# A graph kernel whose last quarter chunk is packed into four columns, and whose last sums and first node groups are handled in another order

## The chip, the cores and the metric

The kernel runs on one core of one Trainium2 chip. The core has five engines that run their own instruction streams: TensorE (PE, matrix multiplies; its weight loads are shown as PEld), VectorE (DVE), ScalarE (ACT), GpSimd (POOL) and SyncE (SP, which here only issues DMAs). Engines wait for each other through semaphores; DMAs are carried by 16 shared DMA engines. The metric is the device time of one execution, in microseconds (us); below, "ns" is written where nanoseconds are meant.

## The reference

A graph network layer over 6250 nodes and 200000 edges with 64 features each; `dst` is sorted, `src` is not.

```python
in_agg = jax.ops.segment_sum(edge_feat, receivers, num_segments=N_NODES)   # by dst
out_agg = jax.ops.segment_sum(edge_feat, senders, num_segments=N_NODES)    # by src
to_updater = jnp.concatenate([in_agg, out_agg, node_feat], axis=1)         # 6250 x 192
h = jax.nn.relu(to_updater @ W1 + b1)                                      # 192 -> 256
x = _layernorm(x + (h @ W2 + b2), axis=-1)                                 # 256 -> 64
```

## The kernel before, in words

Edges are taken in 98 chunks of 2048. A chunk lies in SBUF as 128 partitions by 16 columns of 64 features; the first 1024 edges fill columns 0 to 7 (partition p holds edges 8p to 8p+7), the other 1024 columns 8 to 15. Columns go through the kernel in quads of four. 200000 edges leave 1344 for the last chunk: its first half is full, and of its second half 40 partitions by 8 columns hold the last 320 edges (`LAST_PARTS` is 40); the rest of the half is zeroed features, with node numbers repeated from real edges.

- **Sums by dst** are made by windows: for each half chunk a one-hot matrix of 64 nodes is multiplied by the features on PE (48 matmuls, `sum_windows`), and DVE adds the window to `aggT[0:64]` (`add_window`).
- **Sums by src, directly**: for a quad PE multiplies the features by a matrix of equal node numbers (`same`), so that every edge's row holds the sum over the column's edges of the same node; ACT copies this from PSUM to `payload`, DVE writes row numbers to `target`, and POOL issues one indirect scatter-add DMA for each column (`add_chunk`) into one of four tables in HBM (`out_tab`). The first 2 and the last 18 chunks do this for all four quads, the 78 between for one quad only.
- **Sums by src, shared**: the other 12 columns of the 78 middle chunks are first added into slots (`slot_round`), written to HBM, and read back during the last 18 chunks, where PE adds slot tiles to nodes in seven pairs of node groups (`sum_tiles`, line 1529, 64x64 matmuls with 448 columns). After each pair ACT copies four sums out of PSUM (`flush`) and PE folds them together, one half after the other (`fold`), for ACT to put into `aggT[64:128]` (`put_sums`).

In the last chunk (c = 97, the 18th unit) PE runs, for each of four quads, the next quad's spread of node numbers (line 1491), the 12 matmuls of the quad (lines 1578 and 1580) and some slot tiles; then the windows, and 792 slot matmuls without a break. Then comes the tail, in which nothing is left to overlap with the chunks:

1. SP waits for each table's last scatter-add (`SCATTERED`) and loads its part of node groups 0 and 1 (512 nodes each; there are 12 groups of 512 and one of 106), and then each later group once the sum two groups before has been made.
2. PE folds the last pair: both halves go through the same PSUM bank, so that the second fold waits until ACT has copied out the first (`s_folded`).
3. For each node group g: DVE adds the four tables (`sum_tables`, two instructions), PE transposes the result (`sum_turned`), DVE adds it to `aggT` (`add_tables`, two instructions). PE multiplies by W1: the node's own features (`x_turned`, `hidden_own` in two parts) and the sums (`hidden_sums`); ACT rectifies; PE multiplies by W2 (`outputs`); ACT adds the bias (`biased`); PE transposes back (`back`); DVE adds x and normalizes (line 1389 and on), with the power on POOL, which also issues the store.

The order on each engine is the order in which the code is written. Ahead of the loop over groups stand both parts of `hidden_own` of groups 0 and 1, both `sum_turned`, both `hidden_sums` on PE, and on DVE `sum_tables` and `add_tables` of group 0, the same of group 1, and `sum_tables` of group 2:

```python
for b in range(2):          # DVE
    sum_tables(b, b)
    add_tables(b, b)
sum_tables(2, 0)
```

At the start SP loads the node numbers (`rows_i`, 98 rows of 2048, for src and dst) with four DMAs each, the last row in two pieces (1344 real numbers, 704 repeated ones). ACT turns them to floats for PE to transpose, and DVE takes their minima and maxima.

## Time and profile before

| | |
|---|---|
| median of 3 runs (range) | 1465.55 us (1464.92 to 1467.31) |
| the profiled execution | 1469.09 us, of which the profile spans 1467.2 us |
| PE busy in the span | 1366.5 us (93%) |
| DVE, ACT, POOL busy | 1351.0, 1016.1, 1173.4 us |
| middle chunks (150 to 815 us) | PE busy 652.93 of 665.00 us |
| last 18 chunks, most of them (850 to 1300 us) | PE busy 448.02 of 450.00 us |
| from the last slot matmul to the first layer norm | 1379.30 to 1401.64 us |
| PE busy from 1380 to 1400 us | 14.12 of 20.00 us, mean clock 0.83 |
| layer norm groups, to the last store's issue | 1401.64 to 1459.79 us |

A row of a timeline has the start, the busy time, the engine and line, the operation with output and inputs, and how many instructions were merged; in brackets stands how long the engine had been idle before, and what released it ("issue" is nothing that the profile shows). fp32 matmuls appear as two records each. A row of stretches has, for PE, PEld, DVE, ACT and POOL in this order, the busy time with the number of instructions, then PE's granted clock (1.00 is 2.4 GHz, 0.50 is 1.2 GHz), the busy share of the DMA engines and what they moved in GB/s.

### The profile page before, as it was taken

The numbers are of one execution on the slowest core, as the hardware profiler recorded it, in microseconds if no ns is written. First come the engines' busy times: TensorE is split into PE (matmuls) and PEld (weight loads), VectorE is DVE, ScalarE is ACT, GpSimd is POOL, SyncE is SP. The second block draws the span as 40 slices with busy tenths as digits, with TensorE's granted clock in tenths as the row PEclk, the third lists the DMA queues.
The fourth block names the chain that finished last, engine by engine and source line by source line (L and its number), as shares of the span: only waits on it lengthen the run. The fifth ranks groups of instructions, "written<-read, shape, count | busy, mean of one in ns | idle before, by whom it ended". The sixth has DMA issues, their size and how long they took to land.

```text
span 1467.2 us, 64101 instructions
## 1 busy us (share of the span) xinstructions
PE 1366.5 (93%) x23716; PEld 1064.3 (73%) x23716; DVE 1351.0 (92%) x3564; ACT 1016.1 (69%) x2201; POOL 1173.4 (80%) x667
## 2 busy tenths in 40 slices
PE   3557999999999999999999899999999999999896
PEld 2347999999999999999999566556656565665443
DVE  6987999999999999999999899989999999998576
ACT  6425777777777788887777666776766667676343
POOL 2888888888888888888888688888888888888533
PEclk9969999999999999999999899999999999999998
DMA  9226777777777777779888777776767677666441
GB/s 302 33 15 145 194 194 191 190 195 191 185 185 185 192 195 193 193 192 218 213 211 213 189 181 198 173 186 167 191 166 193 167 185 188 162 172 157 86 129 49
DMA packets 216734, 255.53 MB, mean 174 GB/s; under 512 B 99469, under 2 KB 179356, under 8 KB 216392
## 3 DMA queue, kind: packets, MB, share of 16 engines
q1 hardware_dynamic: 123482, 223.88, 46.7%
q0 software_dynamic: 92960, 28.90, 22.2%
q8 instruction: 105, 1.72, 0.5%
q10 hardware_dynamic: 144, 0.67, 0.2%
q14 instruction: 43, 0.35, 0.1%
HBM read 143.18 MB, written 110.21 MB: 173 GB/s over the span
## 4 chain that ended last, share of the span: by engine, by line
PE 45%; DMA 25%; issue 13%; POOL 12%; DVE 3%; ACT 1%; POOLq 1%; DVEq 0%; ACTq 0%
PE psum L1529 32%; DMA out_tables<-payload,target 24%; POOL out_tables L670 12%; PE psum L1507 3%; PE psum L1676 1%; PE psum L1491 1%; PE psum L1484 1%; PE psum L1580 1%; PE psum L1667 1%; PE psum L1578 1%; PE psum L1688 1%; PE psum L1553 1%; PE psum L1554 1%; DMA cst<-in_consts 1%; DVE to_node L1188 0%
## 5 line engine op out<-in xcount | busy, mean ns | idle before, releaser
L670 POOL DMA_INDIRECT out_tables<-payload,target x632 | 1140.0, 1804 | 223.3 <-issue 187.9
L1507 PE MATMUL psum<-parts,to_slot 128*128 128x194 bf16 x6552 | 589.9, 248 | 7.5 <-ACT slots_out L765 7.5
L1507 PEld LDWEIGHTS psum<-parts,to_slot 128*128 128x128 bf16 x6552 | 555.4, 98 | 24.3 <-issue 8.0
L1529 PE MATMUL psum<-to_node,slots_in 64*64 64x448 bf16 x9828 | 481.2, 351 | 3.3 <-ACT halves_sum L847 2.0
L1529 PEld LDWEIGHTS psum<-to_node,slots_in 64*64 64x64 bf16 x9828 | 284.7, 107 | 178.2 <-DVE to_node L1188 6.1
L765 ACT ACTIVATE slots_out<-psum 128x388 bf16<-128x388 f32 (+1 forms) x936 | 367.5, 474 | 57.0 <-PE psum L1507 49.4
L1149 DVE TENSOR_SCALAR to_slot<-iota_h,slot 128x896 bf16<-128x896 f16 x940 | 377.7, 455 | 0.1
L1188 DVE TENSOR_SCALAR to_node<-iota_h,slot_rel 128x448 bf16<-128x448 f16 x819 | 267.0, 343 | 3.8 <-PE psum L1529 3.2
L1188 DVE TENSOR_SCALAR to_node<-iota_rows,slot_rel 128x448 bf16<-128x448 f16 x546 | 237.1, 434 | 0.0
L784 ACT ACTIVATE payload<-psum 128x256 f32<-128x256 f32 x158 | 61.0, 386 | 207.7 <-PE psum L1580 193.0
L816 ACT ACTIVATE to_node<-apart 128x448 bf16<-128x448 bf16 x273 | 149.0, 575 | 68.3 <-PE psum L1529 67.3
L808 ACT ACTIVATE apart<-iota_h,slot_rel 128x448 bf16<-128x448 f16 x273 | 167.5, 663 | 0.5 <-DVE slot_rel L1160 0.5
L1108 DVE TENSOR_TENSOR rest<-feat,parts 128x1024 f32<-128x1024 f32 x98 | 119.9, 1223 | 22.4 <-ACT parts L744 21.3
L1216 DVE TENSOR_TENSOR same<-psum,cols_code 128x512 bf16<-128x512 f32 x158 | 109.0, 690 | 21.2 <-PE psum L1491 11.7
L1113 DVE TENSOR_TENSOR parts<-rest,parts 128x1024 bf16<-128x1024 f32 x98 | 118.8, 1212 | 1.9 <-ACT parts L754 1.9
L754 ACT ACTIVATE parts<-rest 128x1024 bf16<-128x1024 f32 x98 | 107.5, 1097 | 1.2 <-DVE rest L1108 1.2
L744 ACT ACTIVATE parts<-feat 128x1024 bf16<-128x1024 f32 x98 | 104.5, 1066 | 2.0 <-PE psum L1484 1.9
L1484 PEld LDWEIGHTS psum<-onehot,parts 128*64 128x64 bf16 x4704 | 87.2, 113 | 19.8 <-issue 19.8
L1484 PE MATMUL psum<-onehot,parts 128*64 128x64 bf16 x4704 | 100.8, 198 | 0.0
L1578 PE MATMUL psum<-parts,same 128*128 128x65 bf16 x632 | 79.8, 198 | 13.7 <-issue 8.3
L1580 PE MATMUL psum<-parts,same 128*128 128x64 bf16 x1264 | 84.3, 197 | 0.0
L1578 PEld LDWEIGHTS psum<-parts,same 128*128 128x128 bf16 x632 | 61.0, 100 | 27.4 <-issue 21.6
(129 smaller groups left out, 812.7 us busy)
## 6 DMA issues: line engine op xcount, KB each, us to landing
slot_tiles<-slots_out SPq DMA_DIRECT2D x78, 1018.5 KB
feat<-in_edge_attr SPq DMA_DIRECT2D x195, 256.0 KB
slots_in<-slot_tiles SPq DMA_DIRECT2D x40, 970.0 KB
slots_in<-slot_tiles SPq DMA_DIRECT2D x40, 921.5 KB
out_tables<-payload,target POOLq DMA_INDIRECT x632
out_tables<-zeros POOLq DMA_DIRECT2D x4, 1600.0 KB
feat<-out_tables SPq DMA_DIRECT2D x48, 128.0 KB, 2.2
slots_in<-slot_tiles SPq DMA_DIRECT2D x14, 242.5 KB
```

Source lines behind the costliest of these rows:

```text
L670: e.indirect_dma_start(out_tab, at, payload[b][:, t, :], None, element_offset=k * TABLE_ROWS * D, compute_op=ALU.add).then_inc(s_tab[k], 16)
L765: e.activation(slots_out[b][:, g:g + n, m, :], ps_share[r % BANKS][:, 0:n * SLOT_W].rearrange("p (g w) -> p g w", w=SLOT_W), ACT.Copy).the ...
L808: e.activation(apart[:, n % APARTS, :], iota_h[:, 0:HOT], ACT.Abs, bias=slot_rel[p % RING][:, k:k + 1], scale=-1.0).then_inc(s_apart, 1)
L816: e.activation(to_node[:, node_buf(g, i), :], apart[:, n % APARTS, :], ACT.Relu, bias=1.0, scale=-1.0).then_inc(s_to_node_act, 1)
L1108: e.tensor_tensor(rest[:, :, :], feat[b][:, :, :], parts[b][:, :, 1:1 + D], ALU.subtract).then_inc(s_rest, 1)
L1113: e.tensor_tensor(parts[b][:, :, 1 + 2 * D:1 + 3 * D], rest[:, :, :], parts[b][:, :, 1 + D:1 + 2 * D], ALU.subtract).then_inc(s_lo, 1)
L1149: last = e.tensor_scalar(to_slot[m][:, k, :], iota_h[:, :], slot[:, bass.ds(s, 1), MINI * m + k:MINI * m + k + 1].rearrange("p a k -> p (a ...
L1188: e.tensor_scalar(hot, numbers, slot_rel[p % RING][:, k:k + 1], None, ALU.is_equal).then_inc(s_to_node, 1)
L1484: last = e.matmul(ps_win[b][h], parts[b][:, t, 1 + k * D:1 + (k + 1) * D], onehot[b][:, t // 2, :, t % 2], start=(j == 0 and k == 0), stop ...
L1507: last = e.matmul(ps_share[r % BANKS][:, o:o + SLOT_W], to_slot[m][:, k, g * P:(g + 1) * P], parts[b][:, SHARE_FROM + MINI * m + k, 1:], s ...
L1529: return e.matmul(ps_share[bank_no + h][cols, 0:HOT], slots_in[p % RING][rows, j - PART_FROM[p], D * k:D * (k + 1)], to_node[rows, node_bu ...
L1578: e.matmul(ps_pay[:, o:o + D + 1], w, parts[b][:, t, 0:1 + D], start=True, stop=False)
```

## The change

- The last 320 edges lie in 80 partitions by 4 columns (8 to 11). Columns 12 to 15 of the last chunk hold zeros, and its fourth quad is left out: on PE (12 matmuls and one spread), DVE (`same`), ACT (two copies) and POOL (four scatter-adds). The windows still cover all 16 columns.
- So that the node numbers fit, the last row of `rows_i` is loaded in three pieces: 1024 numbers; 80 times four numbers, each four written twice side by side (a source that is repeated, runs of four numbers, 16 bytes); and 384 repeated ones. That is five DMAs each for src and dst, ten instead of eight.
- The two folds of the last pair go to two PSUM banks (`both`), so that the second no longer waits for the first one's copy.
- In the tail DVE adds the tables of groups 0 and 1 before it adds either to `aggT`, and adds group 2's there too, ahead of the loop. PE has group 0's `sum_turned` between the two groups' `hidden_own`, group 0's `hidden_sums` before group 1's `sum_turned`, group 2's `x_turned` before group 0's `outputs`, and group 2's `sum_turned` right behind it. ACT copies group 2's `x_turned` before `biased` of group 0.

```diff
-LAST_PARTS = (LAST_EDGES - HALF_EDGES) // HALF
-PAD = CHUNK - LAST_EDGES
+LAST_ROWS = (LAST_EDGES - HALF_EDGES) // QUAD
+PAD = (P - LAST_ROWS) * HALF
...
+        FINAL = Mode(0, COLS - QUAD, window=True, sums=True)
...
-        SCATTERED = 16 * ((SHARE_FROM * SHARE_CHUNKS + COLS * (N_CHUNKS - SHARE_CHUNKS)) // OUT_TABLES + 1)
+        SCATTERED = 16 * ((SHARE_FROM * SHARE_CHUNKS + COLS * (N_CHUNKS - SHARE_CHUNKS) - QUAD) // OUT_TABLES + 1)
...
-                chunk(c, c // 2, c % 2, SUMMING, u)
+                chunk(c, c // 2, c % 2, FINAL if is_final(c) else SUMMING, u)
...
-                e.dma_start(rows_i[n][N_CHUNKS - 1:N_CHUNKS, 0:LAST_EDGES], last).then_inc(s_row[n], 16)
-                e.dma_start(rows_i[n][N_CHUNKS - 1:N_CHUNKS, LAST_EDGES:CHUNK],
+                e.dma_start(rows_i[n][N_CHUNKS - 1:N_CHUNKS, 0:HALF_EDGES], last[:, 0:HALF_EDGES]).then_inc(s_row[n], 16)
+                with nc.allow_non_contiguous_dma(reason="the last quarter chunk's rows, four by four"):
+                    e.dma_start(rows_i[n][N_CHUNKS - 1:N_CHUNKS, HALF_EDGES:CHUNK - PAD].rearrange(
+                                    "a (p k j) -> a p k j", k=HALF // QUAD, j=QUAD),
+                                last[:, HALF_EDGES:LAST_EDGES].rearrange("a (p k j) -> a p k j", k=1, j=QUAD).to_broadcast(
+                                    [1, LAST_ROWS, HALF // QUAD, QUAD])).then_inc(s_row[n], 16)
+                e.dma_start(rows_i[n][N_CHUNKS - 1:N_CHUNKS, CHUNK - PAD:CHUNK],
                             last[:, LAST_EDGES - PAD:LAST_EDGES]).then_inc(s_row[n], 16)
...
-                    same_nodes(c, b, c, mode, q)
+                    if q < len(mode.quads):
+                        same_nodes(c, b, c, mode, q)
...
             def group(g, b):
-                biased(g, b)
                 if g == 0:
                     out_of_transposes(2, 0)
+                biased(g, b)
...
-                if g + 2 <= GROUPS:
+                if 3 <= g + 2 <= GROUPS:
                     add_tables(g + 2, b)
...
             for b in range(2):
                 sum_tables(b, b)
+            for b in range(2):
                 add_tables(b, b)
             sum_tables(2, 0)
+            add_tables(2, 0)
...
-                e.wait_ge(s_folded, 2 * g + (h + 1))
-                e.matmul(ps_fold[c % 2], fold_mat[:, :], halves_sum[h][:, :], start=True, stop=False)
-                e.matmul(ps_fold[c % 2], fold_mat[:, :], halves_sum[2 + h][:, :], start=False, stop=True).then_inc(s_fold, 1)
+                both = h if is_last(g) else 0
+                e.wait_ge(s_folded, 2 * g + (h + 1) - both)
+                to = ps_fold[(c + both) % 2]
+                e.matmul(to, fold_mat[:, :], halves_sum[h][:, :], start=True, stop=False)
+                e.matmul(to, fold_mat[:, :], halves_sum[2 + h][:, :], start=False, stop=True).then_inc(s_fold, 1)
```

PE from the two last folds on, before; L1667 is `hidden_own`, L1648 `sum_turned`, L1676 `hidden_sums`, L1688 `outputs`, L1638 `x_turned`, L1696 `back`:

```order
L1553 MATMUL psum<-halves_sum,fold_mat 64x448
L1554 MATMUL psum<-halves_sum,fold_mat 64x448
L1667 MATMUL psum<-parts,w1xx 128x256 x8
L1648 MATMUL psum<-cst,rest 128x128 x4
L1676 MATMUL psum<-aggT,w1io 128x512 x4
L1688 MATMUL psum<-payload,w2s 64x256 x4
L1638 MATMUL psum<-cst,xs 128x128 x4
L1696 MATMUL psum<-cst,onehot 128x128 x2
L1648 MATMUL psum<-cst,rest 128x128 x2
```

The same stretch of PE after the change; L1686 is `hidden_own`, L1667 now `sum_turned`, L1695 `hidden_sums`, L1707 `outputs`, L1657 `x_turned`, L1715 `back`:

```order
L1572 MATMUL psum<-halves_sum,fold_mat 64x448
L1573 MATMUL psum<-halves_sum,fold_mat 64x448
L1686 MATMUL psum<-parts,w1xx 128x256 x4
L1667 MATMUL psum<-cst,rest 128x128 x2
L1686 MATMUL psum<-parts,w1xx 128x256 x4
L1695 MATMUL psum<-aggT,w1io 128x512 x2
L1667 MATMUL psum<-cst,rest 128x128 x2
L1695 MATMUL psum<-aggT,w1io 128x512 x2
L1657 MATMUL psum<-cst,xs 128x128 x2
L1707 MATMUL psum<-payload,w2s 64x256 x4
L1667 MATMUL psum<-cst,rest 128x128 x2
L1657 MATMUL psum<-cst,xs 128x128 x2
```

The same matmuls are issued; group 0's transpose of sums has moved between the two `hidden_own`, group 0's `hidden_sums` ahead of group 1's transpose, and group 2's transposes ahead of and behind `outputs`. DVE in the tail, before; L1358 and L1363 are `sum_tables`, L1377 `add_tables`, L1389 the first row of a group's layer norm:

```order
L1358 TENSOR_TENSOR feat<-feat 128x512
L1363 TENSOR_TENSOR rest<-feat 128x256
L1377 TENSOR_TENSOR aggT<-aggT,psum 64x256 x2
L1358 TENSOR_TENSOR feat<-feat 128x512
L1363 TENSOR_TENSOR rest<-feat 128x256
L1377 TENSOR_TENSOR aggT<-aggT,psum 64x256 x2
L1358 TENSOR_TENSOR feat<-feat 128x512
L1363 TENSOR_TENSOR rest<-feat 128x256
L1389 TENSOR_TENSOR onehot<-xs,psum 128x256
```

And after the change, where L1373 and L1378 are `sum_tables`, L1392 `add_tables` and L1404 the layer norm's first row:

```order
L1373 TENSOR_TENSOR feat<-feat 128x512
L1378 TENSOR_TENSOR rest<-feat 128x256
L1373 TENSOR_TENSOR feat<-feat 128x512
L1378 TENSOR_TENSOR rest<-feat 128x256
L1392 TENSOR_TENSOR aggT<-aggT,psum 64x256 x4
L1373 TENSOR_TENSOR feat<-feat 128x512
L1378 TENSOR_TENSOR rest<-feat 128x256
L1392 TENSOR_TENSOR aggT<-aggT,psum 64x256 x2
L1404 TENSOR_TENSOR onehot<-xs,psum 128x256
```

Both groups' `sum_tables` now stand before the first `add_tables`, and group 2's `add_tables`, which stood inside group 0's layer norm, stands before it.

## Rows read from the trace of the kernel before

**Rows 1.** Stretches: start:end, length, busy per engine, PEclk, DMA share, GB/s.
```profile
850.00:1300.00 450.00, 448.02 (x9304) 272.80 (x9297) 427.65 (x1319) 308.70 (x607) 379.79 (x230) 1.00 0.71 180
```

**Rows 2.** Timeline, PE, last chunk: start, busy, engine, line, operation, count.
```profile
1334.57 0.39 PE L1491 MATMUL psum<-rows_code,ident_bf 98*128 98x512 bf16 x1
1334.80 0.20 PE L1578 MATMUL psum<-parts,same 128*128 128x65 bf16 x1
...
1338.76 0.20 PE L1578 MATMUL psum<-parts,same 128*128 128x65 bf16 x1
...
1339.23 0.59 PE L1553 MATMUL psum<-halves_sum,fold_mat 128*64 128x448 f32 x1
...
1341.65 37.65 PE L1529 MATMUL psum<-to_node,slots_in 64*64 64x448 bf16 x792
```

**Rows 3.** Timeline, POOL, the last scatter-add.
```profile
1379.51 1.55 POOL L670 DMA_INDIRECT out_tables<-payload,target  x1 [0.30 <-issue]
```

**Rows 4.** Timeline, from the last slot matmul to the first fold.
```profile
1379.35 1.85 ACT L847 ACTIVATE halves_sum<-psum 128x448 f32<-128x448 f32 x4 [5.61 <-PE psum L1529]
...
1382.98 0.63 PE L1638 MATMUL psum<-cst,xs 128*128 128x128 f32 x4 [3.68 <-issue]
...
1383.54 1.69 PE L1553 MATMUL psum<-halves_sum,fold_mat 128*64 128x448 f32 x2
```

**Rows 5.** The same timeline, second fold to first layer-norm input.
```profile
1387.30 0.69 DVE L1358 TENSOR_TENSOR feat<-feat 128x512 f32<-128x512 f32 x1 [12.86 <-DMA feat<-out_tables]
...
1387.35 0.97 PE L1553 MATMUL psum<-halves_sum,fold_mat 128*64 128x448 f32 x2 [0.63 <-ACT aggT L854]
...
1389.00 2.67 PE L1667 MATMUL psum<-parts,w1xx 64*128 64x256 f32 x16
...
1391.61 0.44 PE L1648 MATMUL psum<-cst,rest 128*128 128x128 f32 x2
1392.08 0.85 DVE L1377 TENSOR_TENSOR aggT<-aggT,psum 64x256 f32<-64x256 f32 x2 [3.63 <-PE psum L1648]
...
1394.17 0.69 PE L1648 MATMUL psum<-cst,rest 128*128 128x128 f32 x2 [2.13 <-DVE rest L1363]
...
1394.66 4.91 PE L1676 MATMUL psum<-aggT,w1io 128*128 128x512 f32 x8
...
1399.50 1.08 PE L1688 MATMUL psum<-payload,w2s 128*64 128x256 f32 x8
...
1401.64 0.42 DVE L1389 TENSOR_TENSOR onehot<-xs,psum 128x256 f32<-128x256 f32 x1 [4.70 <-PE psum L1696]
```

**Rows 6.** Stretches of 2 us with the granted clock.
```profile
1385.00:1387.00 2.00, 1.72 (x3) 0.23 (x1) 0.00 (x0) 0.24 (x1) 0.00 (x0) 0.50 0.48 141
...
1395.00:1397.00 2.00, 2.00 (x3) 0.68 (x2) 1.86 (x4) 0.33 (x1) 0.00 (x0) 0.50 0.78 230
```

**Rows 7.** The same timeline, start of group 1's tail on PE.
```profile
1405.40 0.41 PE L1638 MATMUL psum<-cst,xs 128*128 128x128 f32 x2 [1.18 <-DVE aggT L1377]
...
1406.08 1.88 PE L1676 MATMUL psum<-aggT,w1io 128*128 128x512 f32 x4
```

**Rows 8.** Chain that ended last, tail: start, us, what.
```profile
1415.85 1.72 PE psum L1676 x4
...
1420.65 1.72 PE psum L1676 x4
```

**Rows 9.** Timeline, start of the kernel.
```profile
9.32 1.91 ACT L732 ACTIVATE rows_f<-rows_i 98x2048 f32<-98x2048 int32 x1 [6.04 <-DMA rows_i<-in_src]
...
13.51 1.91 ACT L732 ACTIVATE rows_f<-rows_i 98x2048 f32<-98x2048 int32 x1
14.01 2.22 DVE L994 TENSOR_REDUCE lowest<-rows_i 98x2 f32<-98x2048 int32 x1
```

**Rows 10.** DMA packets of the first 14 us.
```profile
DMA packets 920, 3.27 MB, mean 233 GB/s; under 512 B 109, under 2 KB 109, under 8 KB 726
```

**Rows 11.** The page's DMA queues (packets, MB, share of 16 engines).
```profile
q0 software_dynamic: 92960, 28.90, 22.2%
```

More of the change, by code:

```diff
@@ L397, in quad_no @@
                 return QUADS * c
-            return c + (QUADS - 1) * FIRST if mode is SHARING else QUADS * c - (QUADS - 1) * SHARE_CHUNKS
+            if mode is SHARING:
+                return c + (QUADS - 1) * FIRST
+            return QUADS * c - (QUADS - 1) * SHARE_CHUNKS - (0 if mode.window else 1)
         def quad_buf(q, b, mode):
@@ L435, in summing_loop @@
                 c = END_SHARE + u
-                chunk(c, c // 2, c % 2, SUMMING, u)
+                chunk(c, c // 2, c % 2, FINAL if is_final(c) else SUMMING, u)
         def sums_before(mode, u):
             for g in range(NODE_PAIRS - 1):
-                if mode is SUMMING and u > 0 and SUM_FROM[u - 1] < (g + 1) * TILES <= SUM_FROM[u]:
+                if mode.sums and u > 0 and SUM_FROM[u - 1] < (g + 1) * TILES <= SUM_FROM[u]:
                     return g
@@ L544, in step @@
                                 slots_out[b][:, :, :, :].rearrange("p g m w -> p g (m w)")).then_inc(s_slot_out[b], 16)
-                if mode is SUMMING:
+                if mode.sums:
                     for k in range(RING, PARTS * NODE_PAIRS):
@@ L1550, in fold @@
                     e.wait_ge(s_wadd, HALVES * (c + 1) + 2)
[L1552 to L1554 removed]
+                both = h if is_last(g) else 0
+                e.wait_ge(s_folded, 2 * g + (h + 1) - both)
+                to = ps_fold[(c + both) % 2]
+                e.matmul(to, fold_mat[:, :], halves_sum[h][:, :], start=True, stop=False)
+                e.matmul(to, fold_mat[:, :], halves_sum[2 + h][:, :], start=False, stop=True).then_inc(s_fold, 1)
             def chunk(c, i, b, mode, at, d=None):
@@ L1708, in group @@
                 if g == 0:
-                    x_turned(2, 0)
+                    sum_turned(2, 0)
                 if g + 3 <= GROUPS:
@@ L1725, in _ @@
                 fold(NODE_PAIRS - 1, m, N_CHUNKS)
-            for b in range(2):
-                for k in range(2):
-                    hidden_own(b, b, k)
-            for b in range(2):
-                sum_turned(b, b)
-            for b in range(2):
-                hidden_sums(b, b)
+            for k in range(2):
+                hidden_own(0, 0, k)
+            sum_turned(0, 0)
+            for k in range(2):
+                hidden_own(1, 1, k)
+            hidden_sums(0, 0)
+            sum_turned(1, 1)
+            hidden_sums(1, 1)
             all_groups(e, group)
```

31 lines of the change are left out of this document (18 added, 13 removed).

## The prediction

> **What bounds the kernel now.** I read the stretches first, since the change touches the start, one chunk near the end and the tail, and each has a limit of its own. In the last 18 chunks PE is the engine that never rests: 448.02 of 450.00 us, at the full clock [rows 1]. So work taken from PE in the last chunk counts in full, and work taken from the others counts only if PE would have waited for it. The timeline of PE shows the last chunk: 792 slot matmuls end the stage without a gap, at 1341.65 + 37.65 = 1379.30 us [rows 2]. POOL, which had issued a scatter-add every 1.55 + 0.30 = 1.85 us, ends its last one at 1381.06 us [rows 3]. That looks like a tie in which the scatters are the later. The next rows decide it: what does each of the two release?
>
> - The scatters release the table loads and so `sum_tables` of group 0 on DVE, at 1387.30 us [rows 5], 6.24 us after POOL's end. But PE takes that sum only at 1391.61 us (L1648), because it is busy with the folds and with 16 records of `hidden_own` until then [rows 5]. The scatter chain ends 1391.61 - 1388.42 = 3.2 us early (`sum_tables` is 0.69 us and a second, smaller instruction, some 1.12 us together by the gap from 1387.30).
> - PE's end releases ACT's four copies (1.85 us) and, after 3.68 us in which PE waits for nothing that the profile shows (it reads the flag and branches), transposes and the first fold at 1383.54 us [rows 4].
>
> So the tail hangs on PE. In it stand two waits that matter. PE waits 0.63 us for ACT to copy the first fold [rows 5]. And at 1394.17 us it has stood 2.13 us for DVE, which does group 0's `add_tables` (0.85 us from 1392.08) and only then group 1's `sum_tables` [rows 5]. Behind this wait the clock is low: 0.50, that is 1.2 GHz, in 1395 to 1397 us, as it was in 1385 to 1387 behind the first pause [rows 6], and the eight records of `hidden_sums` take 4.91 us [rows 5] where four take 1.72 later on [rows 8]. From group 2 on PE sets the pace, one group every 1420.65 - 1415.85 = 4.80 us [rows 8]; this line starts at the `hidden_sums` of 1406.08 us, ahead of which PE waited 1.18 us for DVE's `add_tables` of group 2 [rows 7].
>
> **The change part by part.**
>
> *The quad left out, on PE.* The spread costs 1334.80 - 1334.57 = 0.23 us and the 12 matmuls 1339.23 - 1338.76 = 0.47 us [rows 2]. PE is the bound here, so 0.70 us. Ends: 0, if PE waited for one-hot tiles instead (DVE also loses one `same`, so it doesn't fall behind), and 0.70.
>
> *The quad left out, on POOL.* Four scatter-adds, 4 x 1.85 = 7.4 us [rows 3]. Their end moves to about 1373.7 us and both `sum_tables` become possible before PE's last matmul. What was late was never this chain, so I price it at nothing, with one condition: the new order wants both groups' table sums before group 0's `sum_turned`, some 1.6 us earlier than it stood. With the old scatters DVE would end them at 1387.30 + 2 x 1.12 = 1389.5 us, just at the point of need; the 7.4 us buy certainty there, not time. ACT's two copies and DVE's `same` go from engines that wait for PE: nothing.
>
> *The second bank.* The 0.63 us wait goes [rows 5]. The first fold ran at 1.2 GHz (four records from 1383.54 to the copy, near 3.2 us) and the second at the full clock (1387.35 to 1389.00, 1.65 us) [rows 5, 6]. If the clock rises as late as before, the second fold now begins below it. Ends: the full 0.63, or a loss of 1.65 - 0.63, about 1.0, if all of it runs at half the clock. I take 0.33: less than half of it is slowed, as the clock was back by 1387.35.
>
> *The order of the tail.* Before, from `hidden_own` (1389.00) to the first layer norm row (1401.64) are 12.64 us [rows 5]. Now, counted from `hidden_own`: half of it 1.30; group 0's transpose 0.25 of issue; the other half 1.30, under which DVE's 0.85 is hidden (0.44 + 0.85 against 0.25 + 1.30); `hidden_sums` of group 0 at the full clock 1.72 [rows 8], at 4.57. Group 1's transpose 0.44 and its `add_tables` 0.85 with two handovers of 0.05: 5.95, a wait of about 1 us in place of the 2.13. `hidden_sums` of group 1 1.72, at 7.67; group 2's two transposes about 0.33, at 8.0. `outputs` and what followed took 1401.64 - 1399.50 = 2.14 us [rows 5]; but DVE now has `add_tables` of group 2 ahead of the layer norm: `outputs` 1.01, transpose 0.44, add 0.85 and handover make 2.35. Sum 10.35, so 12.64 - 10.35 = 2.3 us. Of these about 1.3 are the low clock (three of the eight records at 0.86 instead of 0.43 us), the rest is the shorter wait.
>
> *The period's start.* The first layer norm row is then 0.70 + 0.33 + 2.3 = 3.3 us earlier. `add_tables` of group 2 no longer stands inside group 0, and the 1.18 us for which PE waited on it [rows 7] go in part: DVE still is the slower one for a group or two. Between 0 and 1.18 I take 0.6. The line of 4.80 us a group then starts 3.9 us earlier, and all later groups keep their instructions.
>
> *The loads at the start.* Ten DMAs for eight, and in two of them 160 runs of 16 bytes. The src numbers are awaited by ACT (9.32 us), the dst numbers by ACT at 13.51, where it didn't wait, and by DVE at 14.01 [rows 9]; so dst had landed by 13.51, and DVE has 0.5 us to spare. The trace has no such load. The nearest row for a small packet is that of the scatter-adds: 22.2% of 16 engines' 1467.2 us over 92960 packets is 56 ns each [rows 11]. Spread over 16 engines, 10 packets each, that is 0.56 us for one such DMA and 1.1 for both; less 0.5 spare, 0.6 us lost. On one engine it is 160 x 56 ns = 9 us each, 18 us for both. The lower end is 0, if small packets pass beside the large ones. In the first 14 us 109 packets are under 512 B [rows 10], though the single rows of before are runs of 2.8 to 8 KB: single rows are cut up and, most likely, spread. I take a loss of 0.3.
>
> The Trainium skill, "DMA: Bandwidth & Descriptors" (section "Why a DMA increments its semaphore by 16 and not by 1"), says that a DMA uses the largest number of engines up to 16 that divides the slowest dimension of both sides. With 80 or 160 there it would be 16, which speaks for the cheap end. [...] No row of this trace shows on how many engines a load ran.
>
> **Sum.** 0.70 + 0.33 + 2.3 + 0.6 - 0.3 = 3.6 us. The profiled execution took 1469.09 us, so 1465.5 (a span of 1463.6). It lay 3.54 us above the median of the timed runs; the same step from 1465.55 us gives 1462.0 us.
>
> **The rivals.**
>
> - *The clock stays low in the tail.* A pause of about 1 us remains ahead of group 1's `hidden_sums`, and 2.1 us were enough before [rows 5, 6]. Then the 1.3 us come back: 2.3 us gained, 1463.3. For it: the low stretch followed after a busy share of about half. Against it: PE is busy nearly without a break from 1383 on.
> - *The small terms fall short.* The folds bring nothing, DVE keeps the pace of the first groups, the start costs 0.8, the clock stays low: 3.6 - 0.3 - 0.6 - 0.5 - 1.3 = 0.9, 1464.7 us.
> - *The small load is slow.* If the 160 runs go through one DMA engine, dst lands up to 18 us later, src up to 9; DVE, busy without a gap from 14 us on, passes all but 0.5 on to the chunks. Half of the price, 9 us, gives 1465.5 + 8.5 - 3.9 = 1470.2 us. It decides as soon as the delay is over 0.5 + 3.9 = 4.4 us, or 27 ns a packet for both DMAs on one engine. Against it: rows 10.
> - *The scatters were the bound after all.* If the 3.68 us before PE's first transpose are in truth a wait for something on the scatter's side, up to 7.4 - 0.7 more is to be had; with PE then bound by ACT's copies, which end at 1381.20 [rows 4], at most 1382.98 - 1381.20 = 1.8 more: 1460.2 us. Against it: the table sums were 3.2 us early.
>
> **How the numbers follow.** Forecast 0.52; clock 0.20; small terms 0.13; slow load 0.08; scatters 0.07. A change below 0.2%, 2.9 us, can't be told from none by this kernel's runs, which puts the border at 1462.6 us, only 0.6 from the forecast. The forecast's own spread of about 1 us lies three quarters beyond it (0.39), with a quarter of the clock case (0.05) and the last case (0.06): faster 0.50. Slower needs 1468.5 us: 0.08 of the slow load and hardly anything else, 0.08. Same: 0.42. The range leaves out the slow load and part of the ends: 1460.2 to 1465.2 us.
>
> **What would show it.** The row L1529 of 792 ends 0.7 us earlier against the start of the last chunk. POOL's last scatter ends 5 us or more before it. The second L1572 of the last pair shows no wait for ACT. The two `hidden_sums` are apart, with 0.8 to 1.1 us of idle PE between them, and the granted clock from 1390 us on is 1.00. From PE's last slot matmul to the first L1404 are 19.7 us instead of 22.34; the period stays 4.80. At the start, DVE's first reduction stands at 14.0 to 14.6 us. I am wrong if that is past 16 us, if the clock is at 0.50 over 2 us of the tail, or if the gap from the last slot matmul to the first layer norm is as long as before.

## The result, and the profile after

Twelve timed runs each gave 1463.37 us (1460.10 to 1464.94) for the changed kernel and 1466.32 us (1463.58 to 1468.98) for the one before (among its twelve are the three that were known ahead): a ratio of 0.9976, with a 95% interval of 0.9967 to 0.9985, which is 3.5 us (2.2 to 4.8) gained. Forecast were 3.6. The profiled execution spans 1461.7 us instead of 1467.2; these 5.5 us are more than the timed runs show, and the experiments say why.

The last chunk on PE in the profile after (timeline, columns as before) answers to [rows 2]:

```profile
1335.34 0.20 PE L1597 MATMUL psum<-parts,same 128*128 128x65 bf16 x1
...
1339.30 0.59 PE L1572 MATMUL psum<-halves_sum,fold_mat 128*64 128x448 f32 x1
...
1341.72 37.65 PE L1546 MATMUL psum<-to_node,slots_in 64*64 64x448 bf16 x792
```

From the quad's first matmul to the last fold before the windows were 1339.23 - 1334.80 = 4.43 us and are 1339.30 - 1335.34 = 3.96: 0.47 us less, to the digit; the spread's 0.23 us are gone ahead of the quad. The slot matmuls end at 1379.37 us, where they ended at 1379.30. The 0.70 us are there, but this execution was some 0.75 us longer ahead of the last chunks: its first slot matmul stands at 817.97 instead of 817.22 us, though the start is equal (below). In nine profiled executions, those in which the kernel before takes 1466 to 1468 us (of the two kernels and of variants of them), the slot matmuls end between 1377.05 and 1380.50 us, so a span alone can't show 0.7 us.

The tail in the profile after, for [rows 3 to 5] and [rows 7]:

```profile
1373.18 1.55 POOL L683 DMA_INDIRECT out_tables<-payload,target  x1 [0.30 <-issue]
...
1379.67 0.69 DVE L1373 TENSOR_TENSOR feat<-feat 128x512 f32<-128x512 f32 x1 [5.16 <-DMA feat<-out_tables]
...
1380.73 0.68 DVE L1373 TENSOR_TENSOR feat<-feat 128x512 f32<-128x512 f32 x1
...
1382.64 0.63 PE L1657 MATMUL psum<-cst,xs 128*128 128x128 f32 x4 [3.27 <-issue]
...
1383.20 0.96 PE L1572 MATMUL psum<-halves_sum,fold_mat 128*64 128x448 f32 x2
...
1384.75 0.92 PE L1572 MATMUL psum<-halves_sum,fold_mat 128*64 128x448 f32 x2
...
1386.35 1.47 PE L1686 MATMUL psum<-parts,w1xx 64*128 64x256 f32 x8
...
1387.75 0.44 PE L1667 MATMUL psum<-cst,rest 128*128 128x128 f32 x2
...
1389.52 1.98 PE L1695 MATMUL psum<-aggT,w1io 128*128 128x512 f32 x4
...
1391.76 0.86 DVE L1392 TENSOR_TENSOR aggT<-aggT,psum 64x256 f32<-64x256 f32 x2 [2.68 <-PE psum L1667]
...
1392.67 1.98 PE L1695 MATMUL psum<-aggT,w1io 128*128 128x512 f32 x4 [0.95 <-DVE aggT L1392]
...
1397.19 0.42 DVE L1404 TENSOR_TENSOR onehot<-xs,psum 128x256 f32<-128x256 f32 x1
```

PE goes from the first fold into the second without a wait (1383.20 to 1386.35). The table sums, which DVE ended at 1388.4 us and 1394.1 before, are both done by 1381.9, so that the only wait left ahead of a `hidden_sums` is the 0.95 us for group 1's `add_tables`. From the last slot matmul to the first layer norm row are 17.82 us where there were 22.34; the forecast was 19.7. The folds account for 2.0 us of it (3.15 instead of the 5.13 that the forecast implies) and a shorter pause for 0.4 (3.27 instead of 3.68), while the order fell 0.5 short (10.84 instead of 10.35). The folds are short because the clock was up (stretches of 2 us, the granted clock third from the end):

```profile
1383.00:1385.00 2.00, 2.00 (x8) 0.77 (x7) 0.00 (x0) 0.70 (x3) 0.00 (x0) 1.00 0.90 278
...
1391.00:1393.00 2.00, 1.05 (x5) 0.50 (x4) 1.19 (x3) 1.12 (x2) 0.00 (x0) 1.00 0.00 0
1393.00:1395.00 2.00, 2.00 (x8) 0.86 (x8) 0.77 (x2) 1.00 (x2) 0.00 (x0) 1.00 0.09 30
```

It is 1.00 all through the tail. So the four fp32 products of the folds took 3.15 us, at about 0.39 us a record, where the first half of them ran at half the clock before [rows 4, 6]. The period behind is unchanged, 4.80 us a group, in the chain that ended last (start, length, what), as in [rows 8]:

```profile
1410.71 1.72 PE psum L1695 x4
...
1415.51 1.72 PE psum L1695 x4
```

And the start, for [rows 9]:

```profile
9.80 1.91 ACT L745 ACTIVATE rows_f<-rows_i 98x2048 f32<-98x2048 int32 x1 [6.52 <-DMA rows_i<-in_src]
...
13.97 2.29 DVE L1008 TENSOR_REDUCE lowest<-rows_i 98x2 f32<-98x2048 int32 x1 [0.47 <-DMA rows_i<-in_dst]
```

Src numbers came 0.48 us later and dst numbers at least 0.46 (before, ACT didn't wait for them at 13.51 us); DVE stood 0.47 us for them, and its first reduction is where it was, because its work on the constants had begun 0.9 us sooner in this execution. The first matmul of chunk 0 moved by 0.04 us.

### The profile page after: what moved, and what is told of

Same layout as the page of the kernel before. It is cut to its first block, busy times and chain, and to the rows that moved or that the text cites. A ratio compares the mean times of both kernels' runs of the same rounds, so it can differ in the third digit from the quotient of the medians.

```text
span 1461.7 us, 64069 instructions
## 1 busy us (share of the span) xinstructions
PE 1364.3 (93%) x23703; PEld 1062.9 (73%) x23703; DVE 1351.8 (92%) x3563; ACT 1015.8 (69%) x2199; POOL 1164.2 (80%) x663
## 3 DMA queue, kind: packets, MB, share of 16 engines
q8 instruction: 105, 1.72, 0.5%
## 4 chain that ended last, share of the span: by engine, by line
PE 44%; DMA 25%; issue 13%; POOL 13%; DVE 3%; ACT 1%; POOLq 1%; SPq 0%; DVEq 0%; ACTq 0%
PE psum L1546 31%; DMA out_tables<-payload,target 24%; POOL out_tables L683 13%; PE psum L1524 3%; PE psum L1508 1%; PE psum L1501 1%; PE psum L1695 1%; PE psum L1599 1%; PE psum L1686 1%; PE psum L1597 1%; PE psum L1707 1%; PE psum L1572 1%; DMA rows_i<-in_dst 1%; PE psum L1573 1%; DVE to_node L1202 1%
```

## The experiments

Ten variants ran, and the changed kernel twice more, in four groups, each on a chip of its own. Each ratio is against the kernel before on the same chip in the same group. On the chips of the first and third group the kernel before takes 1468 us; on those of the second (banks and order, eight fillers, early flag, the load that can't be cut evenly) and the fourth (late flag) 1519 to 1521 us, so only ratios go across. For the tail three distances are read from each profile, in us: from the last slot matmul to the transposes of x (pause), from the first fold to `hidden_own` (folds), and from there to the first layer norm row (order).

| kernel | ratio (95%) | pause | folds | order | POOL's end against the last slot matmul |
|---|---|---|---|---|---|
| before | 1 | 3.68 | 5.46 | 12.64 | +1.76 |
| changed | 0.9976 (0.9967 to 0.9985) | 3.27 | 3.15 | 10.84 | -4.64 |
| two banks alone | 0.9996 (0.9986 to 1.0006) | 3.34 | 4.84 | 13.17 | +5.60 |
| order alone | 0.9991 (0.9982 to 1.0001) | 3.07 | 5.53 | 11.55 | +5.92 |
| quad out alone | 0.9986 (0.9971 to 1.0001) | 3.12 | 6.37 | 11.63 | -2.42 |
| changed, again | 0.9973 (0.9963 to 0.9984) | 3.33 | 4.85 | 10.84 | -3.96 |
| banks and order | 0.9991 (0.9976 to 1.0006) | 3.53 | 4.35 | 10.85 | -1.77 |
| changed, eight fillers | 0.9968 (0.9954 to 0.9982) | 4.03 | 4.84 | 10.84 | -4.57 |
| changed, early flag | 0.9975 (0.9961 to 0.9989) | 2.99 | 5.68 | 10.84 | -7.01 |
| changed, load as 79 and 1 | 0.9980 (0.9966 to 0.9993) | 3.63 | 5.34 | 10.84 | -6.83 |
| changed, scatters back | 0.9976 (0.9963 to 0.9988) | 3.21 | 3.15 | 17.67 | +6.58 |
| changed, third time | 0.9971 (0.9956 to 0.9985) | 3.60 | 4.85 | 10.84 | +1.61 |
| early flag, 14 fillers | 0.9950 (0.9932 to 0.9967) | 3.07 | 3.15 | 10.83 | -1.95 |
| late flag, 14 fillers | 0.9965 (0.9953 to 0.9978) | 3.76 | 3.15 | 10.84 | -6.34 |

### The three parts, each alone, and the whole

Two banks alone:

```diff
-                e.wait_ge(s_folded, 2 * g + (h + 1))
-                e.matmul(ps_fold[c % 2], fold_mat[:, :], halves_sum[h][:, :], start=True, stop=False)
+                both = h if is_last(g) else 0
+                e.wait_ge(s_folded, 2 * g + (h + 1) - both)
+                to = ps_fold[(c + both) % 2]
+                e.matmul(to, fold_mat[:, :], halves_sum[h][:, :], start=True, stop=False)
```

> The kernel before with the two last folds in two PSUM banks and nothing else. Theory PE (the tail hangs on PE's chain, and the change saves 0.70 us by the quad, 0.3 to 0.6 by the folds, some 2.9 by the order): 0.3 to 0.6 us faster than before; in the profile no wait for ACT between the two folds, the rest of the tail as before, and 22.34 us from the last slot matmul to the first layer norm row become about 21.9. Rival theory clock (what the changed kernel's profile gained beyond the forecast, the folds in 3.15 us instead of 5.46, comes from the change): the folds take 3.2 us here too and 2 us are gained. Rival chance (the clock over the folds differs from execution to execution with no bearing on the change): the folds take 3.2 or 4.8 us, whichever the execution happens to have, and the timed gain stays 0.3 to 0.6.

Measured 0.6 us (a loss of 0.9 to a gain of 2.1). PE's timeline of this run:

```profile
1382.34 1.41 PE L1560 MATMUL psum<-halves_sum,fold_mat 128*64 128x448 f32 x2
...
1385.04 1.46 PE L1560 MATMUL psum<-halves_sum,fold_mat 128*64 128x448 f32 x2
...
1387.18 2.68 PE L1674 MATMUL psum<-parts,w1xx 64*128 64x256 f32 x16
...
1390.14 0.44 PE L1655 MATMUL psum<-cst,rest 128*128 128x128 f32 x2 [0.28 <-DVE rest L1368]
...
1393.00 5.28 PE L1683 MATMUL psum<-aggT,w1io 128*128 128x512 f32 x8
```

The second fold follows without a wait, and the folds take 4.84 us: 0.62 less than before, just the wait. The clock is low in most of them, and again low in `hidden_sums` (5.28 us). So two banks alone don't bring the full clock over the folds. From the last slot matmul to the first layer norm row are 21.91 us, as expected. One thing was not: POOL ended 5.60 us behind the last slot matmul, and PE waited 0.28 us for DVE's table sum. So late scatters can cost time in the old order too.

Order alone (the edits of the tail from the diff above, on PE, DVE and ACT):

```diff
             for b in range(2):
                 sum_tables(b, b)
+            for b in range(2):
                 add_tables(b, b)
             sum_tables(2, 0)
+            add_tables(2, 0)
```

> The kernel before with the new order of the tail on PE, DVE and ACT alone; four columns of scatters more than the changed kernel, one PSUM bank for both folds. Theory PE: 2.3 us sooner at the first layer norm row and 0.6 more by the third group, together 2.9 us; the table sums of both groups end at about 10 us behind the last slot matmul, just as PE wants them, so at most 0.3 of it is lost. Rival scatters (the quad's 7.4 us of scatters are what makes the order pay): group 0's transpose waits for DVE's table sums by 0.5 us or more, and less than 2 us are gained.

Measured 1.3 us (a loss of 0.1 to a gain of 2.6): fewer than the 2.9 expected. The timeline, all engines, and POOL's last scatter:

```profile
1388.30 1.47 PE L1669 MATMUL psum<-parts,w1xx 64*128 64x256 f32 x8
...
1389.04 0.69 DVE L1358 TENSOR_TENSOR feat<-feat 128x512 f32<-128x512 f32 x1 [14.85 <-DMA feat<-out_tables]
...
1390.25 0.44 PE L1650 MATMUL psum<-cst,rest 128*128 128x128 f32 x2 [0.48 <-DVE rest L1363]
...
1392.19 1.98 PE L1678 MATMUL psum<-aggT,w1io 128*128 128x512 f32 x4
```

```profile
1383.41 1.55 POOL L670 DMA_INDIRECT out_tables<-payload,target  x1 [0.30 <-issue]
```

Here POOL ended 5.92 us behind the last slot matmul, and DVE could begin the table sums only at 1389.04 us. PE waited 0.48 us ahead of group 0's transpose. From `hidden_own` to `hidden_sums` are 3.89 us instead of 3.17. That is the rival's wait, at its lower end (it said 0.5 us or more), and less than 2 us were gained, as it said.

Quad out alone (the changed kernel with folds and tail order as before):

```diff
+        FINAL = Mode(0, COLS - QUAD, window=True, sums=True)
...
-                chunk(c, c // 2, c % 2, SUMMING, u)
+                chunk(c, c // 2, c % 2, FINAL if is_final(c) else SUMMING, u)
```

> The kernel before with the last 320 edges in four columns and without the last quad; ten loads of node numbers instead of eight; folds and tail order as before. Theory PE: 0.70 us on PE in the last chunk, 0.0 lost at the start, 0.7 us faster by the clock of the timed runs, 0.4 to 1.0; POOL's last scatter ends 7 us sooner and DVE waits that much less, and nothing follows from it. Rival scatters: the tail from the last slot matmul to the first layer norm shortens by more than 0.5 us beside the 0.70. Rival loads (160 runs of 16 bytes delay the start): DVE's first reduction at 14.5 us or later and the gain of 0.7 eaten.

Measured 2.1 us (a loss of 0.1 to a gain of 4.3), where PE's work is 0.7. The interval holds both. In its profile the clock was low through the folds and most of `hidden_own` (0.50 from 1382 to 1388 us), and then high where it had been low before, though the order is the old one:

```profile
1387.10 3.20 PE L1677 MATMUL psum<-parts,w1xx 64*128 64x256 f32 x16
...
1392.80 0.44 PE L1658 MATMUL psum<-cst,rest 128*128 128x128 f32 x2 [2.13 <-DVE rest L1373]
1393.07 3.60 PE L1686 MATMUL psum<-aggT,w1io 128*128 128x512 f32 x8
```

The same pause of 2.13 us ahead of it, the same eight records, 3.60 us instead of 4.91. This row also gives the old order without the clock: from `hidden_own` to the layer norm 11.63 us here, of which some 0.5 are the slow `hidden_own` (3.13 us to the transpose, where it is 2.61 [rows 5]), so 11.1 at the full clock. The changed kernel again:

> The changed kernel once more, beside its parts. Theory PE: 3.6 us faster than before, and the sum of the three parts (0.7 + 0.45 + 2.9 = 4.05 by the terms) within 1 us of it. Chance: the folds take 3.2 us or up to 4.8, as the execution has it, so that from the last slot matmul to the first layer norm row there are 17.8 us or up to 19.4; theory clock says 17.8 in every profile.

4.0 us gained (2.3 to 5.4); the three parts add up to 0.6 + 1.3 + 2.1 = 4.0. That this fits to the digit is chance: each part is known to 1 or 2 us only, and none of the three by itself is clear of zero. PE in its tail, and a stretch with the clock:

```profile
1381.65 0.63 PE L1657 MATMUL psum<-cst,xs 128*128 128x128 f32 x4 [3.33 <-issue]
...
1382.20 1.33 PE L1572 MATMUL psum<-halves_sum,fold_mat 128*64 128x448 f32 x2
...
1387.05 1.47 PE L1686 MATMUL psum<-parts,w1xx 64*128 64x256 f32 x8
```

```profile
1383.00:1386.00 3.00, 3.00 (x5) 0.92 (x4) 0.60 (x2) 0.54 (x1) 0.00 (x0) 0.50 0.57 173
```

The same program as in the profile after, with folds of 4.85 us instead of 3.15. Its first layer norm row stands 19.57 us behind the last slot matmul, where 19.7 were forecast. From the last slot matmul to the last store were 79.88 us before; they are 74.67 in the profile after and 76.41 in this one, 3.5 us less than before. Of the eleven profiled executions without fillers, two had the full clock over the folds. So about 1.7 of the 5.5 us by which the first two profiles differ belong to the execution and not to the change.

### Are the scatters worth nothing?

Banks and order with the last quad and its scatters kept; the edit is the absence of the changed kernel's first part.

> Folds and tail order of the changed kernel with the last quad and the eight loads of before: the changed kernel without its first part. Theory cover (revised after the parts: in the run of the new order alone POOL ended 5.9 us behind the last slot matmul, the table sums of group 0 and 1 came at 10.0 and 11.07 us, and group 0's sums were taken about 0.7 us late): with the faster folds PE is ready for them at 8 to 10 us, so that PE waits for DVE's table sums ahead of group 0's transpose by 1 to 2 us; the kernel is 1.5 to 2.5 us slower than the changed one: 0.7 by PE's work, the rest by scatters that come late. Theory PE as on record (scatters buy no time): 0.7 us slower than the changed one, 3 us faster than before, no wait ahead of the transpose.

0.9991, against 0.9968, 0.9975 and 0.9980 of the three variants with the quad out in the same group: 1.7 to 3.5 us slower, each interval being 2 us wide to both sides. None of the three is the changed kernel itself. But its profile shows no wait: POOL ended 1.77 us before the last slot matmul, and the table sums were done in time. The cause of the difference is not seen in that execution. So the scatters were put back by themselves, into rows that nothing reads:

```diff
-        SCATTERED = 16 * ((SHARE_FROM * SHARE_CHUNKS + COLS * (N_CHUNKS - SHARE_CHUNKS) - QUAD) // OUT_TABLES + 1)
+        SCATTERED = 16 * ((SHARE_FROM * SHARE_CHUNKS + COLS * (N_CHUNKS - SHARE_CHUNKS)) // OUT_TABLES + 1)
...
-                for t in range(mode.cols):
-                    if t % QUAD == 0:
+                for t in range(COLS if mode is FINAL else mode.cols):
+                    if t % QUAD == 0 and t < mode.cols:
...
+                if mode is FINAL:
+                    ins = e.tensor_copy(target[b][:, n:COLS], spare_row[:, 0:1].to_broadcast([P, COLS - n]))
```

> The changed kernel with four scatter-adds more on POOL at the end of the last chunk, into spare rows that nothing reads, and SP's wait for them; PE, ACT and the loads are as in the changed kernel (DVE writes four target columns more, 0.1 us). It puts back the scatter half of the left-out quad. Theory PE (only the 0.70 us of PE count): no change in time, 0 to 0.3 us slower than the changed kernel. Theory cover (the scatters end late in some executions, by 1 to 6 us behind the last slot matmul, and PE then waits for table sums ahead of group 0's transpose): 0.5 to 1.5 us slower than the changed kernel, and where POOL ends later than 4 us behind the last slot matmul the profile shows DVE's second table sum later than 9.5 us and the first hidden_sums more than 3.2 us behind hidden_own.

> The changed kernel a third time, as the yardstick for the two others of this call: 0.9970 to 0.9980 of the kernel before. Its folds take 4.8 us if the clock falls behind the last slot matmul and 3.15 if not; chance says that the first is the more frequent.

The times don't tell them apart: 0.9976 with the scatters (0.9963 to 0.9988) and 0.9971 without. The profile of the kernel with the scatters, all engines, is that of the slowest of its twelve executions, 1471.79 us; one other took 1470.86, and the rest at most 1465.82:

```profile
1385.53 1.55 POOL L683 DMA_INDIRECT out_tables<-payload,target  x1 [0.30 <-issue]
...
1387.42 1.47 PE L1688 MATMUL psum<-parts,w1xx 64*128 64x256 f32 x8
...
1391.52 0.69 DVE L1375 TENSOR_TENSOR feat<-feat 128x512 f32<-128x512 f32 x1 [15.88 <-DMA feat<-out_tables]
...
1392.73 0.69 PE L1669 MATMUL psum<-cst,rest 128*128 128x128 f32 x2 [3.84 <-DVE rest L1380]
```

The last scatter ended at 1387.08 us, 6.58 behind the last slot matmul; the tables reached DVE at 1391.52, and PE stood 3.84 us ahead of group 0's transpose. Behind that pause the clock was low again: the second half of `hidden_own` took 2.52 us instead of 1.47. Here the scatters set the end, and it cost 24.59 - 17.82 = 6.8 us against the profile after, which has the same folds. POOL's end differs from execution to execution: with the four scatters it was at +1.76, +5.60, +5.92 and +6.58 us in the groups with 1466 to 1468 us, without them at -4.64, -3.96, -2.42, -1.95 and +1.61. The difference of the means, 7.2 us, fits the 7.4 of four scatter-adds. (On the slower chips it was at -1.77 with them and at -4.57 to -7.01 without.) PE begins to wait at about +5.4 if the folds are slow (0.48 us of waiting at +5.92, order alone) and at about +2.7 if they run at the full clock (3.84 us at +6.58). With the scatters the end lies on both sides of these points. Without them the latest was +1.61, in the changed kernel's third run: DVE's sum was ready 1.8 us before PE took it, 0.1 us if the folds had been at the full clock. In all nine profiles with the quad's scatters left out POOL's end lies ahead of these points; that it never passes them is not shown.

### The load of node numbers

```diff
-                    e.dma_start(rows_i[n][N_CHUNKS - 1:N_CHUNKS, HALF_EDGES:CHUNK - PAD].rearrange(
...
+                    for lo, hi in ((0, LAST_ROWS - 1), (LAST_ROWS - 1, LAST_ROWS)):
+                        e.dma_start(rows_i[n][N_CHUNKS - 1:N_CHUNKS, HALF_EDGES + HALF * lo:HALF_EDGES + HALF * hi].rearrange(
...
```

The 80 rows of four numbers, each written twice, become 79 rows in one DMA and one row in another.

> The changed kernel with the 80 rows of the small load taken as 79 and 1, for src and for dst, so that the larger one can't be cut into equal shares. Theory spread (the load in the changed kernel runs on several engines at once, as its dst numbers landed 0.4 us later than before): here the 158 runs go through one DMA engine and dst lands 4 to 18 us later; DVE's first reduction starts at 18 to 32 us instead of 13.97, and the kernel is slower by about as much as that. Rival (small runs are cheap on any engine, or were on one already): reduction at 14 to 15 us and no change in time.

DVE's timeline at the start:

```profile
15.86 2.29 DVE L1010 TENSOR_REDUCE lowest<-rows_i 98x2 f32<-98x2048 int32 x1 [2.61 <-DMA rows_i<-in_dst]
```

The wait for dst is 2.61 us instead of 0.47, and the first matmul of chunk 0 comes at 31.50 us instead of 29.60. Where the time goes is seen at SP, which issues the loads. First the changed kernel's small load of src numbers, then the same of this kernel, the first issue for dst behind it, and the stretch from 8 to 9 us:

```profile
1.84 0.71 SPq L522 DMA_DIRECT2D rows_i<-in_src  x1
```

```profile
1.83 6.71 SPq L523 DMA_DIRECT2D rows_i<-in_src  x2
...
9.04 0.33 SPq L517 DMA_DIRECT2D rows_i<-in_dst  x1
```

```profile
8.00:9.00 1.00, 0.00 (x0) 0.00 (x0) 0.39 (x3) 0.00 (x0) 0.00 (x0) 1.00 0.09 2
```

The DMA of 79 rows took SP 0.83 us, and the one behind it, of a single row, 5.84 us; for dst it was 0.69 and 3.65. SP began with the dst numbers at 9.04 us instead of 3.20 and ended at 14.86 instead of 5.28, 9.6 us later. Most of that was slack: the dst numbers landed 1.9 us later. The time, 0.9980, lies 0.8 us above the early-flag kernel of the same group, which the intervals can't tell from 1.9 or from none. So the load with 158 runs in one DMA costs some 2 us at the start, not 4 to 18. That is no price of a run. The nearest to one is the stretch above: 155 packets under 512 B passed from 8.00 to 9.00 us, one in 6 ns, with hardly anything else moving; that is far below the 56 ns that I took from the scatter-adds. Why SP stood so long in the issue of one row is not shown. The Trainium skill, "DMA: Bandwidth & Descriptors" (section "Why a DMA increments its semaphore by 16 and not by 1"), has the number of engines as the largest divisor up to 16 of both sides' slowest dimension, 1 for 79 rows and 16 for 80. The trace agrees as far as it goes: in that stretch the DMA share is 0.09 of 16 engines, the work of one or two. No row names the engines.

### The pause behind the last slot matmul

Eight matmuls that nobody reads, behind the last slot matmul:

```diff
             summing_loop(e, chunk)
+            e.wait_ge(s_ev, quad_no(N_CHUNKS - 1, FINAL) + len(FINAL.quads) + 2)
+            for _ in range(8):
+                e.matmul(bank[1][:, :], nothing[:, 0:P], iota_h[:, 0:512].bitcast(bf16), start=True, stop=True)
             again = e.value_load(flag_i[0:1, 0:1], min_val=0, max_val=1)
```

> The changed kernel with eight matmuls of 512 columns (1.7 us at the full clock, into a bank that nothing reads) behind the last slot matmul, ahead of the load of the flag. It adds work and takes none away. Theory drain (the 3.3 us behind the last slot matmul are the flag's load and the branch, begun when the queue before them is empty): the transposes come 1.7 us later, at 5.0 us behind the last slot matmul; the folds may run at the full clock (3.15 us instead of 4.8), and the sum is 0 to 1.7 us slower. Theory sequencer (the 3.3 us run from the issue of the last matmul, with the array still working): the fillers are free, transposes stay at 3.3 us, the clock stays at 1.00 over the folds in every profile, and the kernel is about 1 us faster than the changed one.

```profile
1429.81 1.90 PE L1633 MATMUL psum<-iota_h,nothing 128*128 128x512 bf16 x8
1433.90 0.63 PE L1660 MATMUL psum<-cst,xs 128*128 128x128 f32 x4 [2.19 <-issue]
1434.46 1.29 PE L1572 MATMUL psum<-halves_sum,fold_mat 128*64 128x448 f32 x2
```

1.84 us of work made the transposes 0.4 to 0.8 us later (4.03 against the 3.27 to 3.60 of the changed kernel), so neither theory holds alone: more than half of it was hidden, but 2.19 us of idling were left, and the clock still fell. Next the flag's load by itself, earlier:

```diff
+                if is_final(c):
+                    flag.append(e.value_load(flag_i[0:1, 0:1], min_val=0, max_val=1))
...
-            again = e.value_load(flag_i[0:1, 0:1], min_val=0, max_val=1)
+            again = flag[0]
```

> The changed kernel with PE's load of the flag moved from behind the last slot matmul to the start of the last chunk; the branch stays where it was. Theory load (the 3.3 us are mostly the load's latency): the gap behind the last slot matmul shrinks to under 2 us, bounded by ACT's four copies at 1.9 us, and PE shows a pause at the start of the last chunk instead; faster by 0 to 1.5 us. Theory branch (the 3.3 us are the jump over the branch's code): the gap stays over 2.5 us and the kernel is as fast as the changed one or slower by the new pause.

```profile
1432.30 1.09 PE L1661 MATMUL psum<-cst,xs 128*128 128x128 f32 x4 [2.98 <-issue]
```

The pause is 2.98 us, 0.3 to 0.6 less than in the changed kernel, and 0.1 less than in the order alone (3.07): it is mostly not the load. That it is the branch is left by exclusion; no run here leaves the branch out. Then both, with fourteen matmuls, and last the fourteen with the load behind them:

> The changed kernel with PE's flag load at the start of the last chunk and fourteen matmuls of 512 columns (3.0 us, result unread) behind the last slot matmul. In the run with eight fillers the transposes came 4.0 us behind the last slot matmul instead of 3.3 to 3.6, so that 1.0 to 1.3 us of the 1.7 were hidden, and a pause of 2.2 us was left, behind which the clock fell all the same. Theory sequencer: here the pause shrinks below 1.3 us, the transposes come at 4.2 to 4.8 us, the clock stays at 1.00 and the folds take 3.15 us: as fast as the changed kernel or up to 1 us faster. Rival (the pause is as long behind any last matmul): transposes at 5.2 us or later, the clock falls, 1.5 us slower.

```profile
1378.59 3.19 PE L1637 MATMUL psum<-iota_h,nothing 128*128 128x512 bf16 x14
1381.73 0.63 PE L1664 MATMUL psum<-cst,xs 128*128 128x128 f32 x4
1382.29 0.97 PE L1572 MATMUL psum<-halves_sum,fold_mat 128*64 128x448 f32 x2
...
1385.44 1.47 PE L1693 MATMUL psum<-parts,w1xx 64*128 64x256 f32 x8
```

> The changed kernel with the fourteen matmuls behind the last slot matmul, but PE's flag load left where it was, behind them. With the early load the transposes came at 3.07 us, without any pause, and the folds ran at the full clock. Theory load (the early load is what lets the fillers hide: a load of the flag waits until the matmuls before it have ended, and 2.2 us of load and branch follow, as in the run with eight fillers): transposes at 4.9 to 5.3 us, a pause of about 2 us, 1.5 us or more slower than the kernel with the early load. Theory queue (matmuls of 512 columns are long enough for the array to be busy while the sequencer loads and branches, wherever the load stands): transposes at 3.1 to 3.8 us, no pause over 0.5 us, and as fast as with the early load.

```profile
1431.93 3.20 PE L1633 MATMUL psum<-iota_h,nothing 128*128 128x512 bf16 x14
1435.76 0.63 PE L1660 MATMUL psum<-cst,xs 128*128 128x128 f32 x4 [0.63 <-issue]
1436.32 0.97 PE L1572 MATMUL psum<-halves_sum,fold_mat 128*64 128x448 f32 x2
...
1439.47 1.47 PE L1689 MATMUL psum<-parts,w1xx 64*128 64x256 f32 x8
```

With the early load 3.07 us of filler work fit wholly into the pause; with the late one 0.63 us are left, and the transposes come at 3.76 us, 0.2 to 0.5 later than in the changed kernel. That lies by the theory of the queue, not by that of the load (4.9 to 5.3), though its pause is 0.1 us over what was allowed. In both the folds run at the full clock, 3.15 us. The early-flag kernel with fillers takes 0.9950 of the kernel before (0.9932 to 0.9967), beside 0.9971 (0.9956 to 0.9985) of the changed kernel in the same group: medians of 1462.09 and 1464.27 us. It has the lowest ratio of all kernels run; the 2.2 us between the medians (3.1 by the ratios) fit the 1.7 of the clock and some shorter pause, but the intervals overlap a little. The late-flag kernel, with the same full clock, has 0.9965, on another chip.

## Why the prediction was right

The forecast, 3.6 us gained, lies in the measured 2.2 to 4.8, and by the ratio from 1465.55 us the changed kernel takes 1462.0. Point by point:

- *The quad on PE, 0.70.* 0.23 and 0.47 us, as read.
- *The second bank, 0.33.* The wait of 0.63 went in every profile. Whether some of it is paid back by the clock can't be read from single profiles: without fillers the folds took 3.15 to 5.68 us in the eight profiles with two banks, and 5.46 to 6.37 in the three with one. The most frequent value with two banks, 4.84 or 4.85, is 0.61 less than before. If nothing is paid back, the size was 0.3 too low.
- *The order, 2.3.* From `hidden_own` to the layer norm 12.64 became 10.84, the same to 0.01 in every profile of the new order in which POOL wasn't late: 1.8. My 10.35 was 0.5 short: 0.3 in the first step, where two halves of `hidden_own` and a transpose take 3.17 us and not 2.85, because I had halved one merged row and left out the handover between forms, and 0.1 for each `hidden_sums`, which takes 1.82 us until the next work and not 1.72. The split between clock and order was wrong as well. I had 1.3 for the clock and 1.0 for the shorter wait. The wait did shrink from 2.13 to 0.95 us, but the new order gives most of that back by its split `hidden_own` and by group 2's work ahead of the layer norm: against the 11.1 us of the old order at the full clock it gains 0.3. The other 1.5 are the clock, which fell behind the 2.13 us wait in two of three profiles of the old order and in the new one only behind the 3.84 us pause.
- *The period's start, 0.6.* First to third layer norm row 9.33 us before, 8.77 after. From the first row to the last store are 56.85 us, to 0.02, in all profiles of the new order and 57.54 in the three of the old one: 0.69. Right.
- *The start, -0.3.* 0.04 in the first profile; DVE waits 0.24 to 0.55 us for dst in all profiles of this load. Right in kind, small. That it comes from the small runs and not from the two DMAs more is not shown. The slow load's border was miscounted: 4.4 us are 27 ns a packet for the 160 of one DMA, but 14 ns for both DMAs on one engine.
- *The scatters, nothing.* Here the reasoning failed, as a row of one execution stood for all. POOL ended 1.76 us behind PE in the profile I had, and up to 6.6 in others; at the late end PE waits, by 0.28 us in the old order and by 0.48 and 3.84 in the new one. On average over runs it is small: adding them back costs 0.7 us by the ratios, within the noise. The remainder of the 2.1 us of the quad alone stays open.

The terms as measured give 0.70 + 0.63 + 1.8 + 0.69 - 0.04 = 3.8: 0.3 too little for the bank and for the start each stood against 0.5 too much for the order. That the timed gain came within 0.1 of the forecast is luck, as its interval is 1.3 us wide to both sides and 1.5 of the 3.8 hang on a clock that differs from execution to execution. The nine profiles of the new order with POOL in time bear out the mechanism: no wait between the folds, 0.95 us between the two `hidden_sums`, and the full clock over them.

Two of the signs named ahead came out against the forecast, though it held. The clock was to be at 0.50 for less than 2 us of the tail; in the changed kernel's second and third run it was there for 3 us, over the folds. The forecast itself had a slow first fold in it, so the sign was badly chosen. And POOL was to end 5 us or more before the last slot matmul; it did so in none of the three profiles of the changed kernel (-4.64, -3.96, +1.61).

## What to carry to other kernels

Where two chains end within a few microseconds of each other, one profile doesn't say which is late; look at the spread of both ends over several executions before a term is set to nothing. A pause of TensorE behind a long stage can cost twice, once as idling and once as half clock in what follows (folds of 4.85 us instead of 3.15); with the flag loaded early, matmuls that nobody reads filled such a pause here at a cost of 0.1 us. A gain from a new order may be mostly the clock's: count the rows at one level of the clock before you call it the order's. Judge a gain of a few tenths of a per cent by timed runs side by side, not by the span of two profiles, and its parts by distances that are the same in every profile.

## What the runs showed of the hardware that was not expected

- Fourteen matmuls of 512 columns (3.07 us) behind the last useful one fit into the pause that is there anyway: transposes at 3.07 us with them, at 2.99 without them (early load in both).
- The granted clock differed between executions of one program over the same instructions: 1.00 in the folds of one, 0.50 over 3 us of them in two others, behind pauses of 3.27, 3.33 and 3.60 us. It also fell behind pauses of 2.19, 2.98 and 3.07 us, and behind a pause of 2.13 us in two profiles and not in a third. So the length of the pause alone doesn't decide it.
- SP took 5.84 us for issuing a DMA of one row behind a DMA of 158 runs of 16 bytes, where the changed kernel's issues take 0.2 to 0.7 us. The small packets themselves passed at one in 6 ns.
- The same kernel took 1468 us on two chips and 1519 to 1521 on two others, with the tail as long on all: 56.85 us from the first layer norm row to the last store in the new order.
